# Gate's first x products ahead of its statistics, the next key projection ahead of a filler, and the mask beside the taps

## Chip, cores and metric

The kernel runs on one core of a Trainium2 chip. The metric is the time of one execution on the device in microseconds. Five engines work from queues of their own and meet only at semaphores: PE (matmul; its weight loads are listed as PEld), DVE (vector), ACT (scalar), POOL (GpSimd) and SP, which issues most DMA transfers.

## What is computed

The input is 16 sequences of 512 tokens of 256 channels. A token mixer with four heads of 64 channels is followed by a layer norm, a mixture of eight experts (two for each token) and another layer norm. The change lies in the mixer:

```
q, k, v = short_conv(x @ Wq.T), short_conv(x @ Wk.T), short_conv(x @ Wv.T)   # 4 taps, silu
beta    = sigmoid(x @ Wb.T)
# delta rule in chunks: A = -strict_lower(kb k^T); rows solved one by one to T; state S carried on
delta   = delta_rule(q, k, v, beta)
short, long = fir(v, 3 taps), fir(v, 63 taps)
paths   = (short, long, delta, v)
gate_in = concat([x] + [mean and variance per head of each path])
logits  = gelu(gate_in @ gate_w1.T + gate_b1) @ gate_w2.T + bias
probs   = floored softmax over the four paths, per head
out     = rmsnorm(sum_i probs_i * path_i) * w @ Wo.T
```

## The kernel before

Three stages follow each other: stage A (convolutions of v and the long filter, until about 240 us), stage B (the rest of the mixer, the first norm and the routing, until about 1370 us) and stage C (the experts). Stage B works on eight pairs of sequences, 1024 tokens each, and is pipelined over the pairs. Every engine's instruction list is written by hand; the order in it is the order of execution, and semaphore waits are the only coupling.

PE's list for step i: `project(i+1, 0)` (first key projection of the next pair, two matmuls into bank X[0]), behind a hold on `x_out`, the store of the solved blocks; `merges(i)`, which builds the 128-row inverse from 32-row blocks in seven rounds of small matmuls (L881, L897, L904, L919, L928); `solve_rows(i, 0)` (L936); `recur`, the chunk recurrence; `stage1b(i+1)`, with norms, products and selects of the next pair; then `gate(i, b)` for both sequences of pair i, `at_first`, `turn_logits`, `at_rest`. `spin` (L763) multiplies an identity into a bank that nobody reads: it is filler that keeps PE busy. Each fp32 matmul of 512 columns leaves two records in the trace, so "x4" of such a line is two matmuls.

`gate(i, b)` turns the statistics into bank TR (L1004); ACT copies them to `st_t`. Then for each of four groups of 128 hidden units, two x products (L1014) and one statistics product (L1017) add up in X[0] or X[1] by turns, and ACT takes the Gelu (L1321), which frees the bank for the group after next. L1028 and L1040 make the logits.

DVE's list: at the end of `stage1b` the routing of the pair before (`choose`, `place`) and the statistics (`stats`, last line L1679); then `solver(i+1)`, sixty small products and additions in place on `z` (L1527, L1530) and a turned copy (L1534); then `merge_and_mix(i)`: softmax (L1687 to L1710), `weigh` (L1719 to L1721), the three taps of the next key projection (`taps_of(i+2, 0)`, L1462), copies of the merges (L1539) between `add_two` (L1725, L1729), `add_rest` (L1735) and the norm of the mix. `mixd` counts L1721 and L1729.

ACT's list in the same stretch: copies of the at products (L1244) and the exponential (L1250), five loads of the solved blocks that it issues itself (`load_solved`, L1341 and L1345), the first tap of the next projection (`group_a(i+2, 0)`, L1176), then `weigh_values` and its share of the merge copies.

SP stores the solved blocks (`x_out`, `xt_out`) and loads the odd blocks of the inverse, on which the merges wait (L609, `mt_in[0]`); ACT's two even ones count `mt_in[1]`.

POOL's list for a step: `fill_blocks` (zeros above the diagonal of z), `scatter` (sixteen indirect DMAs of the pair before), `mask_at` (one operation over 128 x 4096 of `at_t`, L698). PE's `within(i, 0)` waits for the mask (`at_masked`). `need(eng, sem, value)` leaves out a wait on zero or less.

Of the kernel before, what the change touches and what calls it, by code (L numbers as in the profile page):

```python
# [32 lines left out]
P = 128  # L33
# [5 lines left out]
CH = D // P  # L39
# [10 lines left out]
def need(eng, sem, value):  # L50

    if isinstance(value, int) and value <= 0:
        return
    eng.wait_ge(sem, value)


def hold(eng, sem, value):

    need(eng, sem, value)
    if not isinstance(value, int):  # L60
        eng.nop(nofuse=True)
# [364 lines left out]
def delta_and_gate(nc, t, keep):  # L426

    with ExitStack() as ctx:
# [12 lines left out]
        w1x = sb("w1x", [P, CH, GATE_HID]); w1s = sb("w1s", [3 * STATS, GATE_HID], F32R)  # L441
# [43 lines left out]
        xg = (xg_own[:], ru[:].rearrange("p k b h d -> p k (b h d)"))  # L485
# [5 lines left out]
        X = [ps("x0"), ps("x1")]  # L491
        B2, B3, B4, B5, SM, TR = (ps(n) for n in ("b2", "b3", "b4", "b5", "small", "turn"))

        w_in = sem("weights_in"); pool_c = sem("pool_const"); dve_c = sem("dve_const"); act_c = sem("act_const")
        xa_in, xg_in = sem("xa_in"), [sem(f"xg_in{i}") for i in range(2)]
# [41 lines left out]
        with nc.Block() as block:  # L537
# [114 lines left out]
            def _(pool):  # L652
# [39 lines left out]
                def mask_at(p):  # L692

                    pool.wait_ge(at_kept, 8 * (p + 1))
                    pool.wait_ge(mt_in[1], 32 * (p + 1))
                    pool.nop(nofuse=True)
                    flat = at_t.rearrange("p t h s -> p (t h) s")
                    pool.affine_select(out=flat, in_=flat, compare_op=ALU.is_ge, fill=0.0, base=0,  # L698
                                       pattern=[[0, UNITS], [1, P]], channel_multiplier=-1).then_inc(at_masked, 1)
# [28 lines left out]
            def _(pe):  # L728
                mm = nc.tensor.matmul
# [4 lines left out]
                def project(p, g):  # L734
                    gg = g % 4
                    b, m = gg // CH, gg % CH
                    w = wk if g < 4 else wq
                    if g == 0:
                        pe.wait_ge(xa_in, 16 * (p + 1))
                    if g < 2:  # L740
                        need(pe, gelu_ok, 8 * (p - 1))
                    else:
                        pe.wait_ge(taps, 24 * p + 3 * (g - 1))
                    for c in range(CH):
                        i = mm(X[g % 2][:], w[:, c, m * P:(m + 1) * P], xa[:, c, b * SEQ:(b + 1) * SEQ],  # L745
                               start=c == 0, stop=c == CH - 1)
                    i.then_inc(projected, 1)
# [13 lines left out]
                def spin(bank, n):  # L761
                    for _ in range(n):
                        mm(bank[:], ident[:], wo[:].rearrange("p c n -> p (c n)"), start=True, stop=True)  # L763
# [44 lines left out]
                            if c == 3:  # L808
                                i.then_inc(at_mm, 1)

                def stage1b(p, last=None):

                    if last is not None:
                        pe.wait_ge(x1_kept, 4 * (last + 1))
                    turn_k(p, 0)
                    turn_k(p, 1)
                    turn_norms(p, 0)
                    project(p, 5)
                    for j in (2, 3):
                        pe.wait_ge(k_kept, 4 * p + j - 1)  # L820
                        turn_k(p, j)
                    for j in range(4):
                        b, m = j // CH, j % CH
                        pe.wait_ge(k_kept, 4 * p + j + 1)
                        if j >= 2:
                            pe.wait_ge(kt_kept, 4 * p + j - 1)
                        for q in range(TPB):
                            i = nc.tensor.transpose((B5, B4)[j % 2][:, q * P:(q + 1) * P],
                                                    k_tok[:, b * TPB + q, m * P:(m + 1) * P], ident[:])
                        i.then_inc(k_back, 1)  # L830
                    pe.wait_ge(kt_kept, 4 * (p + 1))
                    for jj in range(4):
                        if jj > 1:
                            for k in a_kept:
                                pe.wait_ge(k, 4 * p + jj - 1)
                        a_products(p, jj)
                    if last is not None:
                        router(last)
                    project(p, 6)
                    pe.wait_ge(beta_ok, 2 * (p + 1))  # L840
                    select(p, 4)
                    project(p, 7)
                    if last is not None:
                        turn_routes(last)
                    for g in range(5, 8):
                        select(p, g)
                        if last is not None:
                            if g == 5:
                                pe.wait_ge(a_kept[1], 4 * (p + 1))
                            spin(B3, 2)  # L850
                    turn_norms(p, 1)
                    if last is not None:
                        rank(last)
                        spin(B3, 3)

                AT_ORDER = (1, 0, 3, 2)

# [140 lines left out]
                def gate(i, b, has_prev, has_next):  # L998
                    half = 2 * i + b
                    if has_prev and not b:  # L1000
                        pe.wait_ge(rt, RT * (i - 1) + 1)
                    pe.wait_ge(st_dve, ST * (i + 1))
                    for j in range(TPB):
                        w = nc.tensor.transpose(TR[0:3 * STATS, j * P:(j + 1) * P],  # L1004
                                                gst[:, b * TPB + j].rearrange("p k s -> p (k s)"), ident[:])
                    w.then_inc(st_turned, 1)
                    pe.wait_ge(xg_in[b], 16 * (i + 1))
                    for c in range(HID_CH):
                        if b == 0 and c == 0:
                            pe.wait_ge(taps, 24 * (i + 2) if has_next else 24 * (i + 1))  # L1010
                        if not (b == 0 and c < 2):
                            pe.wait_ge(gelu_ok, 4 * half + c - 1)
                        for k in range(CH):
                            mm(X[c % 2][:], w1x[:, k, c * P:(c + 1) * P], xg[b][:, k, :], start=k == 0, stop=False)  # L1014
                        if c == 0:
                            pe.wait_ge(st_kept, half + 1)
                        mm(X[c % 2][:], w1s[:, c * P:(c + 1) * P], st_t[:], start=False, stop=True).then_inc(gate_mm, 1)  # L1017

                    pe.wait_ge(gelu_ok, 4 * (half + 1))
                    if b:  # L1020
                        pe.wait_ge(raw_kept, half)
                    elif has_next:
                        for k in a_kept:
                            pe.wait_ge(k, 4 * (i + 2))
                    else:
                        pe.wait_ge(r_ub, 4 * (i + 1))
                    for c in range(HID_CH):
                        w = mm(B2[c * LANE:(c + 1) * LANE, :], w2[:, c, :], hid[:, c, :], start=True, stop=True)  # L1028
                    w.then_inc(raw_mm, 1)
# [80 lines left out]
                    if g > 1:  # L1110
                        select(0, g - 2)
                select(0, 3)
                stage1b(0)
                at_first(0)
                at_rest(0)

                def step(i, has_prev, has_next):
                    if has_next:
                        hold(pe, x_out, 16 * (i + 1))
                        project(i + 1, 0)  # L1120
                    merges(i, has_prev, has_next)
                    pe.wait_ge(m_dve, 9 * (i + 1))
                    solve_rows(i, 0)
                    pe.wait_ge(m_act, 9 * (i + 1))
                    if has_prev:
                        turn_mix(i - 1)
                    recur(i, has_prev, has_next)
                    if has_next:
                        stage1b(i + 1, i - 1 if has_prev else None)
                    else:  # L1130
                        router(i - 1)
                        turn_routes(i - 1)
                        rank(i - 1)
                    for b in range(2):
                        gate(i, b, has_prev, has_next)
                    if has_next:
                        at_first(i + 1)
                    for b in range(2):
                        turn_logits(i, b, has_prev, has_next)
                    if has_next:  # L1140
                        at_rest(i + 1)
                        spin(X[1], 4)
                step(0, False, True)
                with pe.Fori(1, PAIRS - 1) as i:
                    step(i, True, True)
# [1270 lines left out]
```

## Time and profile before

| | |
|---|---|
| three runs | 1894.56, 1901.33, 1901.97 us; median 1901.33 us |
| profiled execution | 1894.72 us, span 1893.0 us |
| mean granted clock of PE | 0.904 |
| busy share of the span | PE 79%, DVE 69%, ACT 50%, POOL 23% |

The span runs from the first to the last instruction; the execution's time lies a little above it. Busy times are averages over three stages with different limits; what matters here are rows of stage B in order of time. In such a row, the first number is the start from the beginning of the span and the second is the time until the end of the last instruction in the row; several equal instructions in sequence are one row with their count; the bracket tells how long the engine stood idle ahead of the row and what released it. Matmuls overlap, so the time between the starts of two rows is the better measure on PE.

### The profile page before, as it was taken

Reading aid. Unit: us, or ns where it says so; the run is one execution under the profiler, and the core shown is the slowest. Engines: PE = TensorE matmul, PEld = TensorE weight load, DVE = VectorE, ACT = ScalarE, POOL = GpSimd, SP = SyncE. Lnnn points to the kernel's source line nnn. Section 1 sums busy time; section 2 is a strip of 40 time slices with the busy share of each in tenths; the row PEclk is TensorE's granted clock in tenths of the full one; section 3 lists DMA queues with packets and bytes.
Section 4 is the critical chain, followed back from the end, with each engine's and each line's share of the span. In section 5 each row is a group of like instructions: output and inputs, shape, how many; then the busy total and the mean of one; then the engine's idle time right before and its main releaser. Section 6 shows DMA issues by size and latency. Waiting matters only on the chain. (4 is left out here: it accounts for less than half of the span.)

```text
span 1893.0 us, 40332 instructions
## 1 busy us (share of the span) xinstructions
PE 1496.2 (79%) x12507; PEld 1108.8 (59%) x12508; DVE 1315.3 (69%) x3331; ACT 950.1 (50%) x1998; POOL 440.7 (23%) x473
## 2 busy tenths in 40 slices
PE   6775165979999999999999999887436999999800
PEld 3445134747747747657557567476225888888700
DVE  6995155677787887887887887875455555554488
ACT  6772061356555644654655555542443555555434
POOL 6884200000030040040030210300223333333300
PEclk9997585989999999999999999998758999999955
DMA  5558642023243243333333333232524533333295
GB/s 197 190 163 256 154 101 58 3 67 94 71 127 92 62 122 102 78 91 101 87 89 106 95 106 90 79 97 76 196 91 140 192 105 101 104 104 101 77 385 190
DMA packets 297370, 224.34 MB, mean 119 GB/s; under 512 B 173472, under 2 KB 265632, under 8 KB 296960
## 3 DMA queue, kind: packets, MB, share of 16 engines
q1 hardware_dynamic: 225600, 158.84, 29.0%
q0 software_dynamic: 15232, 43.53, 6.4%
q10 hardware_dynamic: 56384, 19.93, 4.1%
q8 instruction: 95, 1.56, 0.3%
q14 instruction: 59, 0.48, 0.1%
HBM read 130.42 MB, written 91.82 MB: 117 GB/s over the span
## 5 line engine op out<-in xcount | busy, mean ns | idle before, releaser
L1462 DVE SCALAR_TENSOR_TENSOR B_conv<-B_ps_x,B_cw,B_conv 128x511 f32<-128x511 f32 (+2 forms) x192 | 143.5, 748 | 65.9 <-ACT B_conv L1176 59.3
L2031 POOL DMA_INDIRECT y_d<-C_yb,C_dest x136 | 132.1, 971 | 232.0 <-ACT C_yb L2142 229.7
L422 POOL DMA_INDIRECT xs_d<-x,slot_u x128 | 133.4, 1042 | 137.4 <-DVE m_acc L1857 100.6
L688 POOL MEMSET B_z<- 128x256 f32 (+4 forms) x40 | 5.5, 191 | 674.6 <-DMA B_z<-scr_a 674.6
L1176 ACT ACTIVATE B_conv<-B_ps_x,B_cw 128x512 f32<-128x512 f32 x64 | 43.7, 683 | 167.6 <-PE B_ps_x L745 167.3
L2261 DVE TENSOR_TENSOR C_av<-C_sg,C_ps_g 128x256 f32<-128x256 f32 x136 | 57.3, 421 | 94.6 <-ACT C_sg L2136 94.6
L2065 PE MATMUL C_ps_g<-C_w_high,C_xt_high 128*128 x272 | 119.5, 439 | 0.4 <-issue 0.4
L745 PE MATMUL B_ps_x<-B_xa,B_wk 128*128 128x512 f32 x128 | 67.5, 655 | 63.8 <-DVE B_sel L1454 44.9
L2273 DVE TENSOR_TENSOR C_avt_low<-C_ps_a,C_avt_high 128x256 fp32r<-128x256 f32 x136 | 57.7, 425 | 83.5 <-ACT C_avt_high L2131 83.5
L2065 PE MATMUL C_ps_g<-C_w_high,C_xt_low 128*128 x272 | 107.7, 396 | 0.0
L2065 PE MATMUL C_ps_g<-C_w_low,C_xt_high 128*128 x272 | 107.0, 393 | 0.0
L2136 ACT ACTIVATE C_sg<-C_ps_g 128x256 f32<-128x256 f32 x136 | 52.4, 385 | 107.8 <-PE C_ps_g L2065 107.8
L1527 DVE TENSOR_TENSOR B_zt<-B_z 128x30 f32<-128x30 f32 (+14 forms) x240 | 80.1, 334 | 9.2 <-issue 1.2
L1530 DVE TENSOR_TENSOR B_z<-B_z,B_zt 128x30 f32<-128x30 f32 (+14 forms) x240 | 79.9, 333 | 8.2
L763 PE MATMUL B_ps_x<-B_wo,B_ident 128*128 128x512 f32 x182 | 85.6, 608 | 0.0
L355 DVE SCALAR_TENSOR_TENSOR A_work<-A_ps_x,A_cw,A_work 128x511 f32<-128x511 f32 (+2 forms) x96 | 71.5, 745 | 16.3 <-ACT A_work L308 14.0
L2065 PE MATMUL C_ps_y<-C_w_high,C_avt_high 128*128 x272 | 79.5, 292 | 4.1 <-DVE C_avt_low L2273 3.8
L2142 ACT ACTIVATE C_yb<-C_ps_y 128x256 f32<-128x256 f32 x136 | 52.3, 385 | 60.3 <-PE C_ps_y L2065 57.0
L1321 ACT ACTIVATE B_hid<-B_ps_x,B_b 128x512 f32<-128x512 f32 x64 | 43.9, 688 | 71.9 <-PE B_ps_x L1017 71.8
L936 PEld LDWEIGHTS B_ps_b<-B_ru,area 128*128 128x128 f32 x512 | 67.0, 208 | 21.2 <-issue 12.4
L936 PE MATMUL B_ps_b<-B_ru,area 128*128 128x64 f32 x512 | 68.0, 291 | 12.4 <-DVE area L1539 10.3
L2053 PE MATMUL C_ps_x<-C_ident,C_xb 128*128 128x128 f32 x272 | 52.4, 275 | 31.4 <-DMA C_xb<-xs_d 31.4
(330 smaller groups left out, 4250.6 us busy)
## 6 DMA issues: line engine op xcount, KB each, us to landing
C_xb<-xs_d SPq DMA_DIRECT2D x136, 132.0 KB, 2.1
C_w_high<-y_d SPq DMA_DIRECT2D x12, 1024.0 KB, 14.1
A_band<-fir_long POOLq DMA_DIRECT2D x32, 256.0 KB, 5.9
A_work<-xT SPq DMA_DIRECT2D x16, 512.0 KB, 5.0
v_d<-A_v_tok SPq DMA_DIRECT2D x16, 512.0 KB, 3.5
short_d<-A_sh_tok SPq DMA_DIRECT2D x16, 512.0 KB, 3.2
B_xa<-xT SPq DMA_DIRECT2D x8, 1024.0 KB, 5.8
B_v_tok<-v_d SPq DMA_DIRECT2D x8, 1024.0 KB, 5.5
```

What stands on the lines that cost most here:

```text
L355: nc.vector.scalar_tensor_tensor(conv[:, n % 2, k:], ps_x[n % 2][:, :SEQ - k], cw[:, n % CH, 3 - k:4 - k], conv[:, n % 2, k:], ALU.mult, A ...
L422: pool.indirect_dma_start(t["xs_d"][:, :], bass.IndirectOffsetOnAxis(ap=slot_u[:, c:c + 1], axis=0), x1[:, b, j, :], None).then_inc(done, 16)
L745: i = mm(X[g % 2][:], w[:, c, m * P:(m + 1) * P], xa[:, c, b * SEQ:(b + 1) * SEQ], start=c == 0, stop=c == CH - 1)
L763: mm(bank[:], ident[:], wo[:].rearrange("p c n -> p (c n)"), start=True, stop=True)
L936: w = mm(B2[:, c * DH:(c + 1) * DH], mt[:, (b * TPB + s) * HEADS + h, :], r_sb[:, b, h, :], start=True, stop=True)
L1462: V.scalar_tensor_tensor(conv[:, g % 2, k:], X[g % 2][:, :SEQ - k], cw[:, g // 4, gg % CH, 3 - k:4 - k], conv[:, g % 2, k:], ALU.mult, ALU ...
L1527: V.tensor_tensor(zt[:, 0:left, 0:j], z[:, j + 1:, j:j + 1].to_broadcast([P, left, j]), z[:, j:j + 1, 0:j].to_broadcast([P, left, j]), ALU ...
L1530: V.tensor_tensor(z[:, j + 1:, 0:j], z[:, j + 1:, 0:j], zt[:, 0:left, 0:j], ALU.add).then_inc(solve, 1)
L2031: pool.indirect_dma_start(t["y_d"][:, :], bass.IndirectOffsetOnAxis(ap=dest[:, q:q + 1], axis=0), yb[:, u], None).then_inc(y_out[u], 16)
L2065: w = mm(out, left[lp][:, u, c, :], right[rp][:, bass.ds(e, 1), c, :], start=n_ == 0, stop=n_ == CH * len(PRODUCTS) - 1)
L2261: V.tensor_tensor(av[:, u], sg[:, u], ps_g[u][:, D:GU], ALU.mult).then_inc(act_ok, 1)
L2273: V.tensor_tensor(flat(avt[1]), ps_a[u][:, 0:D], flat(avt[0]), ALU.subtract).then_inc(a_low, 1)
```

## The change

The two x products of the gate's first and second group, for the first sequence of a pair, are issued in `stage1b` of the next pair: the first group's after `select(6)` in place of two filler matmuls, the second group's after `rank` in place of three. The banks X[0] and X[1] hold the partial sums until the gate adds the statistics product. In the last step, without a next pair, the gate does it all as before.

`project(i+1, 0)` no longer waits for `x_out`. The four filler matmuls at the end of a step's list now stand behind the projection at the head of the next step.

`mask_at(p)` no longer waits for ACT's loads of the even blocks; it waits for the first L1721 of the step (`mixd`), and for p = 0 only for the at copies.

```diff
 def mask_at(p):
     pool.wait_ge(at_kept, 8 * (p + 1))
-    pool.wait_ge(mt_in[1], 32 * (p + 1))
+    need(pool, mixd, 4 * (p - 1) + 1)
...
+def hidden_from_x(i, c):
+    pe.wait_ge(xg_in[0], 16 * (i + 1))
+    for k in range(CH):
+        mm(X[c % 2][:], w1x[:, k, c * P:(c + 1) * P], xg[0][:, k, :], start=k == 0, stop=False)
+
-def stage1b(p, last=None):
+def stage1b(p, last=None, first=False):
...
         if last is not None:
             if g == 5:
                 pe.wait_ge(a_kept[1], 4 * (p + 1))
-            spin(B3, 2)
+            if g != 6:
+                spin(B3, 2)
+        if g == 6 and not first:
+            pe.wait_ge(taps, 24 * p + 21)
+            hidden_from_x(p - 1, 0)
     turn_norms(p, 1)
     if last is not None:
         rank(last)
-        spin(B3, 3)
+    if not first:
+        pe.wait_ge(taps, 24 * (p + 1))
+        hidden_from_x(p - 1, 1)
...
 # gate
     for c in range(HID_CH):
-        if b == 0 and c == 0:
-            pe.wait_ge(taps, 24 * (i + 2) if has_next else 24 * (i + 1))
+        if b == 0 and c == 0 and not has_next:
+            pe.wait_ge(taps, 24 * (i + 1))
         if not (b == 0 and c < 2):
             pe.wait_ge(gelu_ok, 4 * half + c - 1)
-        for k in range(CH):
-            mm(X[c % 2][:], w1x[:, k, c * P:(c + 1) * P], xg[b][:, k, :], start=k == 0, stop=False)
+        if b or c > 1 or not has_next:
+            for k in range(CH):
+                mm(X[c % 2][:], w1x[:, k, c * P:(c + 1) * P], xg[b][:, k, :], start=k == 0, stop=False)
...
-stage1b(0)
+stage1b(0, first=True)
...
 def step(i, has_prev, has_next):
     if has_next:
-        hold(pe, x_out, 16 * (i + 1))
         project(i + 1, 0)
+    if has_prev:
+        spin(X[1], 4)
     merges(i, has_prev, has_next)
...
     if has_next:
         at_rest(i + 1)
-        spin(X[1], 4)
```

## Rows read from the trace of the kernel before

**Rows 1.** Timeline of PE in turn 3, from gate to solve_rows.
```profile
804.00 2.82 PE L763 MATMUL B_ps_b<-B_wo,B_ident 128*128 128x512 f32 x6
806.65 0.60 PE L1004 MATMUL B_ps_turn<-B_ident,B_gst 128*96 128x128 f32 x4
...
810.99 1.88 PE L1014 MATMUL B_ps_x<-B_xg,B_w1x 128*128 128x512 f32 x4
...
833.46 3.70 PE L763 MATMUL B_ps_x<-B_wo,B_ident 128*128 128x512 f32 x8
...
838.80 2.21 PE L881 MATMUL B_ps_b<-area 32*32 32x32 f32 x128
...
854.56 3.94 PE L919 MATMUL B_ps_b<-area 64*64 64x64 f32 x64
...
865.60 3.67 PE L936 MATMUL B_ps_b<-B_ru,area 128*128 128x64 f32 x16 [1.31 <-DVE area L1539]
```

**Rows 2.** Timeline of DVE in turn 3: statistics, softmax, taps, first addition.
```profile
804.37 0.28 DVE L1679 COPY B_gst<-B_gst 128x256 f32<-128x256 f32 x1
...
830.14 0.29 DVE L1687 TENSOR_TENSOR B_lg<-B_ps_small,B_bias 128x128 f32<-128x128 f32 x1 [0.67 <-PE B_ps_small L1040]
...
832.54 0.28 DVE L1697 TENSOR_REDUCE B_s<-B_lg 128x32 f32<-128x128 f32 x1 [1.13 <-ACT B_lg L1250]
...
839.88 2.32 DVE L1462 SCALAR_TENSOR_TENSOR B_conv<-B_ps_x,B_cw,B_conv 128x511 f32<-128x511 f32 x3 [1.45 <-ACT B_conv L1176]
...
843.53 2.35 DVE L1725 TENSOR_TENSOR B_lo<-B_lo,B_delta 128x1024 f32<-128x1024 f32 x1
```

**Rows 3.** Timeline of DVE in turn 0: the same addition.
```profile
441.35 1.23 DVE L1725 TENSOR_TENSOR B_lo<-B_lo,B_delta 128x1024 f32<-128x1024 f32 x1
```

**Rows 4.** Timeline of ACT in turn 3: gate, last loads issued, first tap.
```profile
807.99 1.28 ACT L1321 ACT_TABLE_LOAD   x1
809.28 0.69 ACT L1321 ACTIVATE B_hid<-B_ps_x,B_b 128x512 f32<-128x512 f32 x1
...
836.21 1.14 ACTq L1345 DMA_DIRECT2D area<-scr_xt  x2
839.07 0.69 ACT L1176 ACTIVATE B_conv<-B_ps_x,B_cw 128x512 f32<-128x512 f32 x1 [4.43 <-PE B_ps_x L745]
```

**Rows 5.** Timeline of POOL: the mask in turns 3 and 6.
```profile
840.97 3.83 POOL L698 TENSOR_SCALAR_AFFINE_SELECT area<-area 128x4096 f32<-128x4096 f32 x1 [13.65 <-DMA area<-scr_xt]
...
1240.37 3.83 POOL L698 TENSOR_SCALAR_AFFINE_SELECT area<-area 128x4096 f32<-128x4096 f32 x1 [12.66 <-DMA area<-scr_xt]
```

**Rows 6.** Timeline of DVE in turn 6: the first addition.
```profile
1241.20 4.07 DVE L1725 TENSOR_TENSOR B_lo<-B_lo,B_delta 128x1024 f32<-128x1024 f32 x1
```

**Rows 7.** Timelines of ACT and PE in the start-up of stage B.
```profile
288.87 2.09 ACT L1244 ACTIVATE area<-B_ps_b 128x512 f32<-128x512 f32 x4 [0.24 <-PE B_ps_b L806]
...
313.49 2.21 PE L881 MATMUL B_ps_b<-area 32*32 32x32 f32 x128 [1.08 <-DMA area<-scr_xt]
...
318.65 1.56 PE L897 MATMUL B_ps_b<-B_z,B_xf 32*32 32x32 f32 x51 [1.09 <-DMA B_xf<-scr_x]
```

**Rows 8.** Timeline of SP's issues: the merges' loads in turns 3 and 6.
```profile
832.33 0.93 SPq L609 DMA_DIRECT2D area<-scr_xt  x2
...
1234.43 0.93 SPq L609 DMA_DIRECT2D area<-scr_xt  x2
```

**Rows 9.** Timeline of PE in turn 6, from the merges to solve_rows.
```profile
1238.54 2.21 PE L881 MATMUL B_ps_b<-area 32*32 32x32 f32 x128 [0.72 <-DMA area<-scr_xt]
...
1253.28 3.94 PE L919 MATMUL B_ps_b<-area 64*64 64x64 f32 x64
...
1264.97 3.67 PE L936 MATMUL B_ps_b<-B_ru,area 128*128 128x64 f32 x16 [3.28 <-DVE area L1539]
```

**Rows 10.** Timeline of PE in turn 0: L919 and L936.
```profile
452.62 3.94 PE L919 MATMUL B_ps_b<-area 64*64 64x64 f32 x64
...
463.17 1.99 PE L936 MATMUL B_ps_b<-B_ru,area 128*128 128x64 f32 x16 [0.82 <-DVE area L1539]
```

**Rows 11.** Busy time by stretch in turn 1; PEclk is the granted clock.
```profile
595.00:597.00 2.00, 1.02 (x5) 1.03 (x6) 1.97 (x4) 1.97 (x3) 0.00 (x0) 0.62 0.01 4
```

## The prediction, made before the changed kernel ran

> **What bounds the kernel now.** I read the page first, then PE's rows of one turn, then DVE's, ACT's, POOL's and SP's of the same stretch. A turn is the stretch from gate(i) over merges(i+1) to solve_rows(i+1, 0); there are seven of them, 0 to 6, and the numbers are those of turn 3 unless another is named. Between turns the engines hand one chain to each other, so what counts is which wait ends last at each hand-over.
>
> PE's rows stand end to end from the fillers at 804.00 to the merges, which begin at 838.80 without a wait [rows 1]. That is no proof that PE is the bound, since some of it is filler (L763). DVE tells more: it ends the solver before the logits are there and waits 0.67 us for them, then 1.13 us for ACT's exponential, then 1.45 us for ACT's copy of a key projection, and after that its addition at L1725 takes 2.35 us instead of the 1.23 us of turn 0 [rows 2, 3]. After 843 us DVE leads and PE follows: before L936 PE stands 1.31 us for DVE [rows 1]. So up to the first merges PE and ACT hold DVE, and from there to the recurrence DVE holds PE. A gain must come through both.
>
> **The gate.** Now PE runs six filler records from 804.00 to 806.65, turns the statistics, computes x products and statistics product group by group, and starts the third group at 810.99 [rows 1]. ACT copies the turned statistics, loads its table from 807.99 for 1.28 us and starts the first Gelu at 809.28, the moment the table is there [rows 4]. After the change four product records stand where the six fillers did. A record of that shape takes a sixth of 2.65 us, 0.44 us; so the turning starts 2 x 0.44 = 0.88 us earlier, at 805.77. The last statistics are written by 804.65 [rows 2], so DVE doesn't hold it. The other four product records replace four filler records of the same shape behind select(6): nothing lost or won there. In the gate the table load and the first Gelu move to 807.11 and 808.40; the Gelu takes 0.69 us [rows 4], so the bank is free and the third group starts at 809.12 or so, instead of 810.99. The gate's first half ends 1.84 us earlier (half of it from the shorter filler, half because PE waits for ACT instead of computing). The second half is unchanged, so the logits' products end 1.84 us earlier too: a new gap of some 1.5 us on PE behind the first two statistics products is the price, which costs nothing while the clock stays up.
>
> Turn 0 has no fillers behind its selects, so the eight product records fall into PE's waits, and its turning starts no earlier; PE's path there is the gate alone. Bounds are 1.84 - 0.88 = 0.96 us (the half that doesn't come from the filler) and twice 1.77 us (all eight records gone from the gate); I take 1.8.
>
> **Project ahead of the filler.** Filler and projection together fill 833.46 to 838.80 [rows 1]. Their order changes, not their sum. What changes is when ACT gets the projection: its copy started at 839.07 after 4.43 us of waiting [rows 4]. With the projection first, and at_rest 1.84 us earlier, the products end near 833.4 and ACT copies as soon as its own five loads are issued. They follow its last at copy, so 837.35 [rows 4] becomes 835.5, and the tap3 copy is done before DVE's weigh ends. DVE's waits then go: 0.64 of the 0.67 us (the solver ends at 829.5 by the wait's start), some 0.7 of the 1.13 us (ACT's at copies come earlier, the exponential itself stays), all of the 1.45 us. DVE reaches the taps 2.8 us earlier. The wait for x_out itself costs nothing in the loop: filler, projection and merges stand without a gap.
>
> **The mask.** POOL's mask takes 3.83 us from 840.97 [rows 5]. It overlaps L1725 from 843.53 to 844.80, 1.27 us, and L1725 grows by 1.12 us [rows 2, 3]. In turn 6 the overlap is about 3.0 us and L1725 takes 4.07 us, 2.84 more [rows 6]. So this DVE addition, which reads two SBUF tiles, does almost nothing while the mask runs, whereas the taps (one operand in PSUM) kept their 2.32 us although the mask began under the last of them [rows 2]. With the new wait, the mask starts when weigh's third product is done: now 1.45 us ahead of the taps, 838.43 [rows 2], after the change near 837.1. It then lies under taps and the PSUM copies of merge(0) and ends about 841.0 to 841.5, when L1725 is due at 840.8. At most half a microsecond of contention is left. On POOL, only the next fill_blocks is queued behind it, some 90 us later: nobody waits.
>
> At the start, need() with a negative value waits for nothing, so mask_at(0) starts with the last at copy, at 290.96 [rows 7], while solver(0) runs, whose products and additions also read two SBUF tiles. No row shows a solver operation beside a mask: the cost lies between 0 and 3.83 us, and by the nearest row, L1725 in turn 6, it is 2.84/3.0 of the mask, 3.6 us. The first merges wait for that solver's result, the next ones have 1.09 us of slack on another load [rows 7], which now goes out without waiting for the projection. So start-up loses 3.6 - 1.1 = 2.5 us. The Trainium skill (SBUF — State Buffer, Who interferes with whom) says that a VectorE operation with two SBUF inputs and a GpSimd operation that reads SBUF shut each other out entirely. By that rule the start-up would lose 3.8 - 1.1 = 2.7 us, by the row 2.5, and the sum would be 0.2 us smaller; the trace agrees for L1725, and for the solver no row shows it.
>
> **What is late next.** Two things cap the gain per turn. First, merges(i+1) needs SP's loads of the solved odd blocks: issued at 832.33 in turn 3 [rows 8]; in turn 6 they were issued at 1234.43 and PE's wait for them ended at 1238.54, 4.1 us later [rows 9]. By that, turn 3's load is there at 836.4 and PE is ready at 838.80 - 1.84 = 836.96: hidden by half a microsecond. But ACT's loads also start 1.84 us earlier, into the same DMA engines, and in turn 6 PE waits already, so nothing is won there ahead of the merges. For turns 1 to 5 I take 1.5 us out of 0 to 1.84.
>
> Second, from L919 on, PE's products at L919 feed DVE's copies, and DVE's rest follows. Turn 0, whose L1725 was not blocked, needs 10.55 us from L919 to L936, turn 3 11.04 [rows 1, 3, 10]. So of DVE's larger lead only up to 0.49 us more arrives; I take 0.4 for turns 1 to 5. Turn 6, with the longest block, needs 11.69 us [rows 9]; 1.14 less is 10.55, so I take 1.1 (bounds 0 and the block's 2.84).
>
> **The clock.** In turn 3 L936 takes 3.67 us, in turn 0 1.99 us [rows 1, 10], because after such a gap the granted clock falls: in turn 1 to 0.62 on average of the stretch around L936, which is part 2.4 and part 1.2 GHz [rows 11]. The gap in turn 0 is 0.82 us, and the clock held. The forecast gap in turns 1 to 5 is 1.31 - 0.49 = 0.82 us as well, but one turn is no proof. Bounds are 0 and 6 x 1.68 = 10 us; I take 2.
>
> **Sum.** Turn 0 1.8; turns 1 to 5, 5 x (1.5 + 0.4) = 9.5; turn 6 1.1; clock 2; start-up -2.5: 11.9 us. The profiled execution took 1894.72 us (span 1893.0), so 1883 us. The median shown, 1901.33, lies 6.6 us above it and the spread of three runs is 7.4 us; a measurement of this kernel can't tell less than about 0.5%, 9.5 us, from no change.
>
> **Rivals.**
> *The load becomes the bound* (chance 0.2). ACT's earlier loads delay SP's, and the merges start when they did. Turns 1 to 5 then keep 0.4 each, and the clock's 2 us go, since PE has a gap more: 1.8 + 2 + 1.1 - 2.5 = 2.4 us, 1892. For it: turn 6 waits already. Against: half a microsecond of cover in turn 3.
> *The clock holds in all turns* (0.17). The full 10 us instead of 2: 1875. For it turn 0; against, only one turn shows it.
> *The early products don't shorten the gate* (0.11). If the first Gelu doesn't move, DVE's cleared waits and the mask are left, but PE's row ahead of the merges keeps its length: 0.5 in turn 0, 5 x (0.4 + 0.4), 1.1, clock 2, start-up -2.5, together 5.1: 1890. Against it: ACT stood idle ahead of the turning.
> *Slower: the clock falls in the gate's new gap* (0.08). The gap is 1.5 us, longer than the 1.31 us ahead of L936 after which it fell. Half clock over the third and fourth group's x products, 1.77 us each, costs up to 3.5 us a turn against 1.84 won; the logits end up to 1.7 us later, all of it ahead of the merges, and with the start-up, and the mask's 0.2 a turn back, the loss is 7 x 1.5 + 2.5 - 2 = 11 us: 1906. It decides if the stretch behind the gap shows a clock below 1. Against it: the gap lies between 512-column products, that of L936 between small ones.
> The forecast keeps 0.44.
>
> **Range.** From 1870 (clock rival with 4 us for the unknown turns) to 1894 (the load rival with its bounds); the slower case and some of the edges are left out, 2 in 10. Faster by over 0.5% means below 1885 on the profile's scale: most of the forecast, 0.38, the clock rival, 0.17, and 0.05 of the others, 0.6; slower 0.07; the rest 0.33.
>
> **What would show it.** In the profile after: the first additions at L1725's place all at 1.2 to 1.7 us; the mask beginning before the taps; ACT's first Gelu 1.5 us after the statistics' copy ends with no PE wait behind it; DVE's waits for logits and for ACT's tap3 copy gone; the merges 7.8 us behind the end of the solver (829.47) instead of 9.3; the first solver 3.6 us longer. I am wrong if PE waits for the loads ahead of the merges in most turns, if the gate's third group doesn't start earlier, or if the clock is below 1 in the gate.

## The result, and the profile after

The changed kernel takes 1914.47 us in the median of four runs (1910.84 to 1915.58), the kernel before 1901.38 (also four runs, 1894.56 to 1901.97). The ratio is 1.0085, 95% interval 1.0057 to 1.0113: slower by 0.85%, where 0.6% faster had been forecast. The profiled execution took 1913.99 us, span 1912.2, mean granted clock 0.897; before, the span was 1893.0 and the clock 0.904.

Lines of the changed kernel lie 11 to 12 further down: L881 is L892, L919 L930, L936 L947, L1014 L1026, L1725 L1737; the early x products are L814. First the timeline of PE in turn 3, which answers to [rows 1] (start, duration, engine, line, operation; in brackets the idle time before it and what ended it):

```profile
815.91 0.60 PE L1015 MATMUL B_ps_turn<-B_ident,B_gst 128*96 128x128 f32 x4
817.27 0.73 PE L1029 MATMUL B_ps_x<-B_st_t,B_w1s 96*128 96x512 f32 x2 [0.76 <-ACT B_st_t L1329]
819.27 3.68 PE L1026 MATMUL B_ps_x<-B_xg,B_w1x 128*128 128x512 f32 x4 [1.27 <-ACT B_hid L1333]
...
826.91 0.65 PE L1015 MATMUL B_ps_turn<-B_ident,B_gst 128*96 128x128 f32 x4
...
842.43 1.16 PE L806 MATMUL B_ps_b<-B_q_t,B_k_t 64*128 64x128 f32 x16 [0.28 <-ACT area L1256]
846.14 3.24 PE L745 MATMUL B_ps_x<-B_xa,B_wk 128*128 128x512 f32 x4 [2.54 <-issue]
849.17 4.08 PE L763 MATMUL B_ps_x<-B_wo,B_ident 128*128 128x512 f32 x8
853.18 2.21 PE L892 MATMUL B_ps_b<-area 32*32 32x32 f32 x128
...
868.93 3.94 PE L930 MATMUL B_ps_b<-area 64*64 64x64 f32 x64
...
879.48 2.45 PE L947 MATMUL B_ps_b<-B_ru,area 128*128 128x64 f32 x16 [0.82 <-DVE area L1551]
```

Two places are new. Behind the last product of at_rest (L806, which ends at 843.59) PE stands idle for 2.54 us, and what ends the wait is called issue: the profile shows neither a semaphore nor a transfer that PE waited for. Then the projection takes 3.24 us where it took 1.88, and the fillers 4.08 where they took 3.70 [rows 1]. From at_rest's end to the merges it is 853.18 - 843.59 = 9.6 us; before, 838.80 - 833.46 = 5.3 [rows 1]. The other place is the gate: the third group's products (819.27) take 3.68 us, twice 1.88, behind two gaps of 0.76 and 1.27 us. The granted clock by stretch (the last three columns are PEclk, DMA share, GB/s) shows the lower level in both places:

```profile
818.00:820.00 2.00, 0.73 (x2) 0.40 (x2) 1.79 (x7) 1.78 (x3) 1.42 (x2) 0.85 0.28 101
820.00:822.00 2.00, 2.00 (x5) 0.77 (x3) 1.83 (x6) 0.00 (x0) 1.60 (x2) 0.50 0.28 101
...
846.00:849.00 3.00, 2.86 (x4) 1.26 (x5) 2.50 (x3) 0.00 (x0) 0.37 (x1) 0.62 1.17 183
```

Over 820 to 822 us the clock is 0.50, 1.2 GHz, and over 846 to 849 a mixture of both levels. The view of waits over turns 1 to 6 (engine, tile, line, releaser: us in total, times, longest) counts the issue wait:

```profile
PE B_ps_x L745 <- issue: 14.5, 5, 3.2
```

Five times: in turns 1 to 5, at 3.19, 2.92, 2.54, 3.24 and 2.63 us. Turn 0 and turn 6 don't have it. PE is TensorE, and its list has a loop over steps 1 to 6; these five are just the places where its program branches back from the end of one step to the head of the next. In the kernel before, the last instructions of the loop's body were the four fillers (eight records).

The other engines in turn 3, as timelines of ACT, POOL and DVE ([rows 2, 4, 5]):

```profile
849.58 0.69 ACT L1188 ACTIVATE B_conv<-B_ps_x,B_cw 128x512 f32<-128x512 f32 x1 [4.87 <-PE B_ps_x L745]
...
848.63 3.83 POOL L698 TENSOR_SCALAR_AFFINE_SELECT area<-area 128x4096 f32<-128x4096 f32 x1 [11.21 <-DVE B_sh L1733]
...
840.21 0.29 DVE L1699 TENSOR_TENSOR B_lg<-B_ps_small,B_bias 128x128 f32<-128x128 f32 x1 [0.63 <-PE B_ps_small L1052]
...
850.40 2.31 DVE L1474 SCALAR_TENSOR_TENSOR B_conv<-B_ps_x,B_cw,B_conv 128x511 f32<-128x511 f32 x3 [1.91 <-ACT B_conv L1188]
...
855.86 1.23 DVE L1737 TENSOR_TENSOR B_lo<-B_lo,B_delta 128x1024 f32<-128x1024 f32 x1
```

The mask does what was forecast: it begins ahead of the taps and the first addition takes 1.23 us. But the projection comes so late that ACT waits 4.87 us for it and DVE 1.91 for ACT.

Where the span's 19.2 us went, by the starts of solve_rows (L936 before, L947 after) in the eight pairs: the first is 6.1 us late (2.0 of that are there before anything that changed has run), turn 0 wins 2.9, turns 1 to 6 lose 16.8. Of these, the stretch from at_rest to the 64-row products loses 21.2 us and the gates' first half 4.4; the stretch from the 64-row products to solve_rows wins 2.5, and that from solve_rows to the next gate 6.3. Behind turn 6 another 0.8 us comes back.

### The profile page after: what moved, and what is told of

Read it like the earlier page. It is cut to its first block and busy times, and to the rows that moved or that the text cites. A ratio compares the mean times of both kernels' runs of the same rounds, so it can differ in the third digit from the quotient of the medians.

```text
span 1912.2 us, 40219 instructions
## 1 busy us (share of the span) xinstructions
PE 1489.5 (78%) x12447; PEld 1104.6 (58%) x12448; DVE 1312.7 (69%) x3331; ACT 950.4 (50%) x1998; POOL 438.7 (23%) x473
## 5 line engine op out<-in xcount | busy, mean ns | idle before, releaser
L2077 PE MATMUL C_ps_y<-C_w_high,C_avt_low 128*128 x272 | 76.2, 280 | 0.0
L2077 PE MATMUL C_ps_y<-C_w_low,C_avt_high 128*128 x272 | 76.1, 280 | 0.0
```

Of the source, the lines that this page charges most:

```text
L2077: w = mm(out, left[lp][:, u, c, :], right[rp][:, bass.ds(e, 1), c, :], start=n_ == 0, stop=n_ == CH * len(PRODUCTS) - 1)
```

## The experiments

Each was timed against runs of the kernel before on the same chip; ratios are to those, with their 95% intervals. Three theories of the loss were held against each other. Theory 1: TensorE's branch back, which had run under the fillers, now leaves the engine idle. Theory 2: the clock falls in the gate's new gaps. Theory 3: the earlier loads and the mask at the start-up cost the time.

**The change's three parts.** The order alone, on the kernel before:

```diff
 def step(i, has_prev, has_next):
     if has_next:
-        hold(pe, x_out, 16 * (i + 1))
         project(i + 1, 0)
+    if has_prev:
+        spin(X[1], 4)
     merges(i, has_prev, has_next)
...
         at_rest(i + 1)
-        spin(X[1], 4)
```

> The kernel before with nothing changed but the order of projection and filler, and the projection's hold left out. Theory 1, the loop: PE's list goes back to the head of its loop between the at products and the projection, and without the filler at the end of the loop's body PE stands still for 2.5 to 3.2 us there in each of five turns, with a low clock behind it; the merges then begin about 9.7 us behind the at products instead of 5.3, and the kernel takes 15 to 20 us longer than before. Theory 2, the gate: the loss of the changed kernel comes from the low clock in the gate's gap; then this kernel is within 4 us of before. Theory 3, the loads and the start-up mask: also within 4 us of before.

Measured: 1918.68 us, ratio 1.0100 [1.0073, 1.0126]. The issue gap stands in turns 1 to 5 with 2.80 to 3.48 us, and the gates are those of before (10.18 us in the first halves of these turns):

```profile
PE B_ps_x L745 <- issue: 15.4, 5, 3.5
```

This part alone loses as much as the whole change, as theory 1 had it.

The mask alone, on the kernel before:

```diff
-    pool.wait_ge(mt_in[1], 32 * (p + 1))
+    need(pool, mixd, 4 * (p - 1) + 1)
```

> The kernel before with nothing changed but the mask's wait. All theories: the first addition of each turn takes 1.23 us, and L919 to L936 takes 10.55 us in turns 1 to 5. Theory 1 and 2: the first solver is 3.7 us longer, the turns give back 0.4 us each in turns 1 to 5 and about 1 us in turn 6, so the kernel is 0 to 2 us longer than before, which this measurement can't tell from nothing. Theory 3: the start-up alone costs 5 us or more and the kernel is at least 5 us longer.

Measured: 1895.57 us, 0.9981 [0.9963, 1.0000]. In turns 0 to 5 the first additions take 1.23 us, and L919 to L936 takes 10.55 us with a gap of 0.82. L936 itself took 1.99 us in three of these turns, and 2.25 to 3.66 in the other three. The kernel is no longer than before, against theory 3; the 0 to 2 us of loss that was expected did not show either.

The gate alone is the changed kernel without the two other parts:

```diff
 # in the changed kernel
     if has_next:
+        hold(pe, x_out, 16 * (i + 1))
         project(i + 1, 0)
-    if has_prev:
-        spin(X[1], 4)
...
         at_rest(i + 1)
+        spin(X[1], 4)
...
+    pool.wait_ge(mt_in[1], 32 * (p + 1))
-    need(pool, mixd, 4 * (p - 1) + 1)
```

> The kernel before with nothing changed but the gate's first products. Theory 1: the gate's first half takes 9.3 us where the clock holds and 10.8 to 11 us where it falls, against 10.2 us before, and begins 0.9 us earlier; the kernel is within 5 us of before on either side. Theory 2: the clock falls in most turns and the kernel takes 10 us longer or more. Theory 3: no more than 3 us from before.

Measured: 1891.81 us, 0.9960 [0.9939, 0.9981]. The first halves of the gates take 9.2 to 9.3 us in four turns, 9.84 in turn 6, and 10.9 to 11.0 in the other two. The gain, some 7.5 us (3.6 to 11.6), is above the 5 us that theory 1 had allowed on either side, though not beyond its interval; theory 2's loss of 10 us is ruled out.

The three ratios add up to 0.4% slower where the whole change is 0.85% slower; the intervals are just wide enough for both to be the same.

**The fillers back at the loop's end,** in the changed kernel; the projection keeps its place at the head, without its hold:

```diff
         project(i + 1, 0)
-    if has_prev:
-        spin(X[1], 4)
...
         at_rest(i + 1)
+        spin(X[1], 4)
```

> The changed kernel with its four filler matmuls put back at the end of the loop's body; the projection follows them without its hold. Theory 1: no idle time of PE ahead of the projection, the merges 5.3 us behind the at products, and 15 to 20 us less than the changed kernel, so within 5 us of before. Theory 2: the gate still falls to the low clock, and the kernel stays 10 us or more above before. Theory 3: the loads still go out early and the start-up is the same, so it stays 5 to 10 us above before.

Measured: 1885.76 us, 0.9924 [0.9898, 0.9951]. PE's timeline in turn 3 has no gap:

```profile
828.50 1.16 PE L806 MATMUL B_ps_b<-B_q_t,B_k_t 64*128 64x128 f32 x16 [0.27 <-ACT area L1255]
829.60 3.70 PE L763 MATMUL B_ps_x<-B_wo,B_ident 128*128 128x512 f32 x8
833.13 1.88 PE L745 MATMUL B_ps_x<-B_xa,B_wk 128*128 128x512 f32 x4
834.94 2.21 PE L892 MATMUL B_ps_b<-area 32*32 32x32 f32 x128
```

By the ratios this is 1.6%, some 30 us, less than the changed kernel, more than the 15 to 20 us expected. In the profiled executions 21.5 us of it lie between at_rest and the 64-row products, so the fillers' place cost most of the time. Another 6.1 us lie in the gates' first halves, of which two of seven ran partly at the lower clock instead of five; what decides which of them do is not shown. Whether it is the branch that costs, or the projection that is slow to begin at that place, the next two tell apart.

**The loop written out,** in the changed kernel, order unchanged:

```diff
-with pe.Fori(1, PAIRS - 1) as i:
+for i in range(1, PAIRS - 1):
     step(i, True, True)
```

> The changed kernel with one edit: TensorE's loop over turns 1 to 5 is written out as five copies, so that its program has no branch back between at_rest and the projection; the order of the projection, the filler and the merges is the changed one. The other engines keep their loops. Theory 1 (the branch back of TensorE's loop is what stands idle): the idle time named issue ahead of the projection, 2.5 to 3.3 us in turns 1 to 5, is gone, the projection starts within 0.3 us of at_rest as in turn 0, and the time is about that of the version with the filler back at the loop's end, 1886 us, 1880 to 1892, ratio to before 0.989 to 0.996. Rival A (the place of the projection itself costs it: its wait for x_out, or TensorE fetching the projection's weights): the issue gap stays at 2.5 to 3.3 us and the time at 1914. Rival B (the branch's cost only moves to other code that has to be loaded, as the program is longer): other issue gaps of together 2 to 3 us appear in each turn, 1905 to 1920 us.

Measured: 1885.53 us, 0.9939 [0.9920, 0.9959]. The projection follows at_rest at once, in turn 3 as in the others:

```profile
832.35 1.16 PE L806 MATMUL B_ps_b<-B_q_t,B_k_t 64*128 64x128 f32 x16 [0.27 <-ACT area L1256]
833.44 1.98 PE L745 MATMUL B_ps_x<-B_xa,B_wk 128*128 128x512 f32 x4
```

From at_rest's end to the merges it is 5.3 to 5.4 us again in turns 0 to 4, with the projection first. A single issue wait is left, 1.42 us within the first merges of turn 4: the branch's cost has not just moved to other places in each turn.

**Half the fillers at the end:**

```diff
     project(i + 1, 0)
     if has_prev:
-        spin(X[1], 4)
+        spin(X[1], 2)
...
         at_rest(i + 1)
+        spin(X[1], 2)
```

> The changed kernel with two of the four filler products behind at_rest at the loop's end and two behind the projection. A filler product of this form takes about 0.9 us at 2.4 GHz. Theory 1 (the branch back takes a fixed time of some 3 us, which queued products cover as long as they run): the two fillers cover some 1.8 us, so that the issue gap ahead of the projection is 0.7 to 1.5 us in turns 1 to 5, and the time lies between 1914 and 1886: about 1895, 1888 to 1903. Rival A (any product behind at_rest is enough, since it is the queue's emptiness and not a length of time that costs): no gap, 1884 to 1889. Rival B (the gap is set by something of the projection's own): the gap stays at 2.5 to 3.3 us behind the fillers, 1912 to 1918.

Measured: 1894.53 us, 0.9984 [0.9966, 1.0001], between the two, as theory 1 has it. PE in turn 3, and the issue wait of turns 1 to 5:

```profile
837.71 1.98 PE L763 MATMUL B_ps_x<-B_wo,B_ident 128*128 128x512 f32 x4
840.40 1.98 PE L745 MATMUL B_ps_x<-B_xa,B_wk 128*128 128x512 f32 x4 [0.70 <-issue]
```
```profile
PE B_ps_x L745 <- issue: 4.9, 5, 1.3
```

The mean gap falls from 2.90 to 0.98 us, by 1.92, and the two fillers take 1.98. So what costs is a length of time, 2.5 to 3.2 us here, and queued products cover it one for one; that the queue is not empty is not enough.

What lies beside it shows in the view of transfers. One microsecond around at_rest's end, of the changed kernel in turn 3:

```profile
DMA packets 2, 0.02 MB, mean 16 GB/s; under 512 B 1, under 2 KB 1, under 8 KB 1
## 3 DMA queue, kind: packets, MB, share of 16 engines
q8 instruction: 1, 0.02, 6.0%
```

The same microsecond behind at_rest in the kernel before, where the fillers run:

```profile
q8 instruction: 1, 0.02, 6.0%
```

This queue is of the kind instruction. Its packet starts between 0.1 us ahead of at_rest's end and 0.6 behind it in all five turns of the changed kernel, and 0.3 to 1.0 behind it in the kernel before; a second follows 3.8 to 4.7 us behind at_rest's end. In the written-out kernel the stretch from 2 us ahead to 3 us behind holds none in turns 1 to 4. Over the whole execution q8 has 95 packets in both kernels and 86 where TensorE's loop is written out, while writing out VectorE's and ScalarE's loops in a later version leaves it at that version's 93: so the queue goes with TensorE's list. The reading that fits is that the branch back fetches code, and that with fillers in PE's queue nobody sees it. That much is inferred: the packet itself takes about 1 us, and no row shows what the rest of the gap is spent on.

**A control: the loop written out in the kernel before.**

> A control: the kernel before with TensorE's loop over turns 1 to 5 written out, nothing else. There the filler at the end of the loop's body covers the branch back, so nothing of it shows. Theory 1 (only an uncovered branch costs): no change, ratio to before 0.998 to 1.002. Rival (a program written out is faster for another reason, so that the gain of the written-out changed kernel says nothing of the branch): 12 to 28 us faster, ratio 0.985 to 0.994.

Measured: 1893.76 us, 0.9956 [0.9934, 0.9977]. This is as neither side had it: 0.44% faster, a third of what the step is worth in the changed kernel. All of turns 0 to 5 need 10.47 us from L919 to L936 there, and the gap ahead of L936 is 0.74 us where it was 0.82 to 1.38. So a written-out list saves something besides an uncovered branch. One part of it shows in the rows: the mask begins 6.1 to 6.9 us behind at_rest in turns 1 to 5, before 7.1 to 8.1, and the first additions, which it holds up, take 1.23 to 1.77 us there instead of 2.00 to 2.98. Why the loads that the mask waits for are there earlier stays open. The proof by the written-out kernel is weaker by this, that by the fillers is not.

**Versions meant to beat both.** The next projection at the tail of the loop's body, ahead of the fillers; the first mask with its old wait:

```diff
-    need(pool, mixd, 4 * (p - 1) + 1)
+    if isinstance(p, int) and p == 0:
+        pool.wait_ge(mt_in[1], 32)
+    else:
+        need(pool, mixd, 4 * (p - 1) + 1)
...
-def step(i, has_prev, has_next):
-    if has_next:
+def step(i, has_prev, has_next, has_after):
+    if has_next and not has_prev:
         project(i + 1, 0)
-    if has_prev:
-        spin(X[1], 4)
...
         at_rest(i + 1)
+        if has_after:
+            project(i + 2, 0)
+        spin(X[1], 4)
...
-with pe.Fori(1, PAIRS - 1) as i:
-    step(i, True, True)
+with pe.Fori(1, PAIRS - 2) as i:
+    step(i, True, True, True)
+step(PAIRS - 2, True, True, False)
...
```

> A version meant to beat the changed kernel: the next pair's projection stands at the tail of the loop's body ahead of the four fillers, so that projection goes ahead of the filler as in the changed kernel, and the fillers cover the branch back; and the first mask (start-up) keeps its old wait, the later ones the new one. Theory 1: no issue gap ahead of the projection, the projection follows at_rest directly, the fillers end where the merges may begin; the time is that of the version with the filler back at the loop's end, 1886, less what the earlier projection frees, which can only be where ACT's copies of it (B_conv) are waited for last: 0 to 0.9 us a turn, so 1880 to 1886; the start-up mask's price of 3.7 us on DVE is gone, but the merges there waited 26 us for a transfer of scr_xt anyway, so 0 to 2 us of it: 1883, 1876 to 1888. Rival (the projection ahead of the filler costs what the filler had covered of at_rest's turnings, so later copies): 1886 to 1893.

Measured: 1883.25 us, 0.9925 [0.9904, 0.9947]: as forecast, and not to be told from the version with the fillers back. The next version is the same with a filler product in each of the gate's two gaps:

```diff
 if c == 0:
+    if b == 0 and has_next:
+        spin(B3, 1)
     pe.wait_ge(st_kept, half + 1)
 mm(X[c % 2][:], w1s[:, c * P:(c + 1) * P], st_t[:], start=False, stop=True).then_inc(gate_mm, 1)
+if b == 0 and c == 1 and has_next:
+    spin(B3, 1)
```

> The version of tail_mask0 with a filler product in each of the gate's two new gaps on TensorE: one 128 x 512 product ahead of the wait for the statistics' copy and one behind the second group's last product, in the first half of each gate that has a next pair. Theory 2 (the gate's products run at the lower clock level behind these gaps, which costs some 1.7 us in four to five of seven turns): the first half of the gate takes 9.2 to 9.9 us in all turns where it took 11 in some, and the time is 5 to 9 us below tail_mask0, 1872 to 1879. Rival A (the filler itself stands on the path, 0.2 to 0.9 us each, as the statistics' copy comes before it ends): the gate's half takes 9.6 to 10.3 in all turns, 0 to 3 us below tail_mask0. Rival B (the clock falls all the same): 11 us in some turns and 0.4 to 1.8 more in each, so 3 to 10 us above tail_mask0.

Measured: 1883.37 us, 0.9924 [0.9899, 0.9949]. PE in turn 3:

```profile
804.93 0.60 PE L1018 MATMUL B_ps_turn<-B_ident,B_gst 128*96 128x128 f32 x4
805.36 1.02 PE L766 MATMUL B_ps_b<-B_wo,B_ident 128*128 128x512 f32 x2
806.29 0.73 PE L1034 MATMUL B_ps_x<-B_st_t,B_w1s 96*128 96x512 f32 x2
806.86 1.02 PE L766 MATMUL B_ps_b<-B_wo,B_ident 128*128 128x512 f32 x2
808.29 1.98 PE L1029 MATMUL B_ps_x<-B_xg,B_w1x 128*128 128x512 f32 x4 [0.41 <-ACT B_hid L1342]
```

The products keep the full clock, and the first half takes 9.2 to 9.3 us in turns 0 to 5 and 9.84 in turn 6, where the version before took 10.8 to 11.6 in six of seven. The clock falls behind the gaps, and filling them holds it: theory 2's mechanism is right. But the time didn't move, where 5 to 9 us less had been expected. In the profiled executions solve_rows of turn 6 starts 5.1 us earlier; of the 9.6 us won in the gates, 3.7 went in the stretches from solve_rows to the next gate, where the products of solve_rows ran at the lower clock more often, and 3.4 us more behind turn 6. A gain of a few us can't be told from none here.

The branch on the other engines, in the version with the gaps filled; the same edit is made in ScalarE's list (act):

```diff
-with dve.Fori(1, PAIRS - 2) as i:
+for i in range(1, PAIRS - 2):
```

> The version with the gate's gaps filled, with the loops of VectorE and ScalarE over turns 1 to 4 written out as well. VectorE's rows of before and after show idle time named issue, 1.7 to 2.05 us, ahead of the first batch norm statistics behind the loop's head, four times in all, and ScalarE's one of 2.1 to 3.0 us behind its loop's exit. Theory 1 widened to the other engines: these gaps go (below 0.3 us), in all four turns. What that is worth: between 0, as VectorE waits for TensorE's recurrence there anyhow, and 4 x 1.8 + 2.5 = 9.7 us; I take 2, so ratio to before 0.991, 0.986 to 0.9945. Rival (the gap on VectorE is not the branch, but the time of its batch norm's start or of a transfer): the gaps stay, and so does the time, ratio 0.990 to 0.995.

Measured: 1883.77 us, 0.9896 [0.9863, 0.9929]. DVE (VectorE) at its loop's head in turn 3:

```profile
859.17 1.23 DVE L1767 TENSOR_TENSOR B_lo<-B_lo,B_r 128x1024 f32<-128x1024 f32 x1
860.31 3.23 DVE L1589 BATCH_NORM_STATS2 B_bn<-B_v_tok 128x6 f32<-128x128 f32 x16
```

The gap that was 1.75 to 2.0 us is gone in all four turns, so it was the branch; ScalarE's stayed (2.85 us), so that was not. The time shows no gain beyond its interval: four gaps of 1.8 us on DVE were worth nothing that can be measured. The gates' first halves take 9.84 to 10.12 us in turns 1 to 5 there, instead of 9.3. With TensorE's loop written out as well:

> The previous version (tail projection ahead of the fillers, first mask with its old wait, gate's gaps filled, VectorE's and ScalarE's loops written out) with TensorE's loop over turns 1 to 5 written out as well. Theory 1 alone (the fillers cover TensorE's branch already): no change to the version before it, ratio 0.987 to 0.993. Rival (a written-out TensorE loop saves something besides the branch, as the kernel before became 0.4% faster by it, 8 us): 4 to 8 us more, ratio 0.983 to 0.989, with the products of solve_rows starting 10.47 us behind the 64-row products instead of 10.55.

Measured: 1881.49 us, 0.9922 [0.9898, 0.9946]: no more, though the 10.47 us of the rival are there in turns 0 to 5. Six versions lie between 1881 and 1886 us, by ratio 0.990 to 0.994, and cannot be told apart; the one with the fillers back gets there by moving the fillers alone, without a written-out list.

## Why the prediction was wrong

**Filler and projection: "Their order changes, not their sum".** This step failed. The sum went from 5.3 us to 9.6 to 10.3 in turns 1 to 5, 4.6 more in the mean: 2.9 of idle time for the branch, and some 1.7 because the projection and the fillers behind it run partly at 1.2 GHz (in turn 3, 1.36 and 0.38 us). Five turns make 23.1 us, less 0.8 in turn 6 and 1.1 for stalls of the kernel before, ahead of and within the merges, that went: the 21.2 above. The order as such costs nothing: in the written-out kernel, with the projection first, the sum is 5.3 to 5.4 us in turns 0 to 4, as forecast. I read in [rows 1] that filler and projection stand without a gap and took the filler for dead weight that can stand anywhere; I had not asked what the loop's last instruction covers. The trace of before held the answer in the view of waits, on DVE, whose loop has no filler at its end:

```profile
DVE B_bn L1568 <- issue: 7.2, 4, 2.0
```

Four waits for nothing that the profile shows, 1.8 us each, at the head of VectorE's loop. The Trainium skill says it too (Runtime: NRT & Kernel Launch, Instruction fetch mechanics): a taken branch whose target lies outside the code at hand has to wait until it is fetched. The traces agree that there is such a wait, and give its price: 2.5 to 3.5 us on TensorE, 1.7 to 2.1 on VectorE.

**Everything else summed to about what was forecast, in part by luck.** With the fillers back at the loop's end the other parts give 0.76% less (0.49 to 1.02), 14.4 us of 1901.33 where I had 11.9. Its profiled execution, the fastest of six, took 1880.12 us where I had 1883; its span is 14.6 us shorter than that of before. By stretches, the start-up lost 5.2 us where I had 2.5; turn 0 won 2.4 (I had 1.8), turns 1 to 5 won 12.0 and turn 6 3.9 (9.5 and 1.1, with 2 for the clock between them), and 1.6 came from behind turn 6, where I had nothing. So the sum agrees to 2.7 us because 5.4 us won beyond the forecast met 2.7 us lost beyond it. By parts:

- The gate. At the full clock the first half takes 9.2 to 9.3 us; 10.18 less the forecast 0.96 is 9.22. The rest of the 1.84 us is the earlier turning. But in the changed kernel five of seven gates ran partly at 1.2 GHz and took 10.8 to 12.8. The rival on this clock, held at 0.08, named the mechanism rightly and its price too high: some 1.7 us a gate in turns 1 to 5, which takes the gain back and no more, where I had 1.5 us of net loss a turn. The kernel came out slower, as this rival had it, but by the loop's end and not by the gate. With the fillers back two of seven gates have it, and the kernel is faster.
- The mask. First additions 1.23 us in turns 0 to 5, 10.55 us from L930 to L947 and a gap of 0.82, the forecast values. In turn 6 the addition kept 3.70 us and the gap 3.28; the 1.1 us there came to 0.35.
- The clock behind that gap. My 2 of 10 us was a guess from one turn. After gaps of the same 0.82 us it held in some turns of 0 to 5 and fell in others: the products of solve_rows took 1.99 us in five turns and 2.83 in one with the fillers back, 1.99 to 3.15 in the changed kernel, up to 3.66 with the mask alone.
- The start-up. The timelines of DVE, POOL and PE:

```profile
293.09 4.07 DVE L1542 TENSOR_TENSOR B_z<-B_z,B_zt 128x220 f32<-128x220 f32 x1
...
293.07 3.85 POOL L698 TENSOR_SCALAR_AFFINE_SELECT area<-area 128x4096 f32<-128x4096 f32 x1 [8.43 <-ACT area L1256]
...
320.00 3.62 PE L892 MATMUL B_ps_b<-area 32*32 32x32 f32 x128 [26.28 <-DMA area<-scr_xt]
```

One solver operation of 0.39 us takes 4.07 beside the mask, 3.68 lost, where 3.6 was forecast from the row of turn 6. The Trainium skill's rule on the pair (SBUF — State Buffer, Who interferes with whom) gives the whole mask, 3.8; the trace lies between. The 1.1 us of slack that I set against it did not help: SP's load is issued 3.9 us behind the start of the solver's last copy, as before, and the merges begin 4.5 us behind that issue instead of 3.6. The first solve_rows starts 4.1 us later (6.1 less the 2.0 that were there already), not 2.5.
- DVE's waits. I had those for logits and for ACT's copy gone, and 0.7 of the 1.13 us for the exponential. In turns 1 to 6 the first and the last shrank with the fillers back (six waits for logits became two; 6.8 us for the exponential became 4.3). That for ACT's copy stayed at 1.2 to 1.5 us in turns 1 to 5, as the projection stood behind the fillers again.
- The load as the bound did not come in turns 1 to 6 of the changed kernel; turn 0 waited 0.71 us for it there, and 1.40 with the gate alone; in the written-out kernel turn 5 waited 1.70.

## What to carry to other kernels

Before filler is moved away from a loop's end, ask what it covers: a branch back left an engine idle for 1.7 to 3.5 us here unless enough work was queued ahead of it, and the profile shows it only as issue at a loop's head, on whichever engine has no such cover. Not every wait for issue is a branch: with the projection at the loop's tail, ACT shows 2.9 to 3.9 us of it ahead of its first tap in turns 0 to 5, where it issues its own loads, and issuing is not counted as busy. Move the useful step, and leave the filler last: the projection ahead of the fillers at the loop's tail keeps both. A part that is right by its own rows can be lost under one that isn't, so time the parts alone.

## What the hardware showed that was not expected

- A branch back on TensorE with nothing queued ahead of it left 2.5 to 3.5 us of idle time, with one packet of some 0.02 MB on an instruction queue beside it; two filler products of 1.98 us together hid 1.92 us of it.
- TensorE's clock fell to 1.2 GHz behind two gaps of 0.76 and 1.27 us in the gates of turns 1, 2, 3 and 5, and not in turn 4 with the same gaps (first halves of 10.8 to 11.0 us, and 9.31); in turn 6 it fell behind gaps of 0.68 and 1.88 us. A filler in each gap kept it up in all seven gates; in the products of solve_rows it then fell more often.
- With TensorE's loop written out the kernel was 0.44% faster [0.9934, 0.9977] even where the branch was covered.
